# Where a language-model tower prepares its FFN weights: raw loads into the bytes of the result, in-place mixing, the token chain first, and half of the turning moved into FFN block 0

## The chip, the cores and the metric

One NeuronCore of one Trainium2 chip. The metric is the device time of one execution in microseconds; the median of three runs is given. The profiled execution is a run of its own, with its own time.

## The reference, cut to what matters

16 rows of 256 token ids below 128 go through one tower. All ids come from a table of 128 rows, so everything up to the attention scores depends on the table alone.

```python
h = rms(rms(emb[x], norm_weight) @ proj.T)                    # token part: 128 distinct rows
y = layernorm(h);  q, k, v = y @ Wq.T, y @ Wk.T, y @ Wv.T     # 16 heads of 32
q, k = layernorm(q*gamma + beta), layernorm(k*gamma + beta)   # per head
attn = tril((q k^T / sqrt(32)) ** 2)
h = h + (attn @ v / (rowsum(attn) + 1e-5)) @ Wo.T
x = fwht512(layernorm(h) * SU_ug) / 64                        # Walsh-Hadamard transform
x = silu(x @ W_gate.T * ws_g) * (x @ W_up.T * ws_u)           # W_gate, W_up: 2048 x 512
x = fwht2048(x * SU_dp) / 64
h = h + x @ W_down.T * ws_d                                   # W_down: 512 x 2048
```

## The kernel before

The 4096 tokens are eight blocks of 512. Work is written as five instruction streams (SP issues loads, POOL, DVE, ACT, PE), and each stream's order is written out by hand. Semaphores named in the code order the streams against each other; a stream that waits holds back all that is behind it.

**Preparation.** SP loads the weights. PE turns (transposes) the 128x128 tiles of `proj`, Wq, Wk, Wv, Wo with `small_unit` (20 units of four tiles; each unit goes through one PSUM bank and is copied by ACT with `small_copy`, in two banks `TURN_SMALL` used in turn). The token part, q, k and v of the 128 rows, and the scores follow; ACT squares the scores and writes their high fp16 half, DVE the low half (`att`). Every fp32 weight of the large products is kept as two fp16 halves, so a product is three matmuls (`split_mm`, lines 1009 to 1011).

W_gate and W_up are eight groups of 512 rows, 32 units of four tiles. A group first needs the sums of squares of its rows (`gu_squares` on ACT, line 778: four 128x512 squares), `gu_norm` (DVE), a power on POOL (line 302), `gu_scale` (DVE, which also builds a diagonal matrix), and then PE multiplies the raw tiles with that diagonal (`turn_unit`, line 1004), ACT copies the high half (line 781) and DVE subtracts to get the low half (`unit`, line 438). W_down is mixed along its 2048 columns by four butterfly stages on DVE for each of its four row groups (`down_mix`, 16 mixes, each two `tensor_tensor` of 128x1024 at lines 410 and 411, from one buffer to another), turned (`down_turn`, 16 units), multiplied with a 128x128 Hadamard matrix (`down_hada`, line 1040) and split into halves (`down_unit`).

**Slots.** A block's attention is 32 slots and its FFN is 32 slots. In attention slots 0 to 15 each slot handles one head: PE picks (`PICK`, lines 1138, 1139), DVE multiplies with the counts (`product`, line 633), ACT writes the high half, POOL the low half (line 337). After heads 3, 7, 11, 15 (slots 4, 8, 12, 15, `SUMS_AT`) PE sums over four heads (line 1153), DVE divides (lines 642 to 651), ACT and POOL split, and a slot or two later PE flips the result and ACT copies it (`oT`). From slot 18 on PE multiplies with Wo; per 128 tokens DVE adds the residual (line 675), takes the norm, mixes by butterflies (lines 687, 410, 411), ACT and DVE split (`x16`, line 660), PE flips and applies the Hadamard matrix, ACT and DVE split again into `xT` (line 667). FFN slots 0 to 15 compute gate and up (`feed_half`), slots 16 to 31 the product with W_down (`feed_down`).

Block 0's attention runs alone, with the units and mixes of the weights between its slots (`UNITS_IN_SLOT`, `DOWN_MIX_AT`). After it, block b's FFN runs beside block b+1's attention: FFN block 0 is written out (with the 16 `down_turn` and 16 `down_hada` in its slots 0 to 8), blocks 1 to 6 are a hardware loop on each engine, and FFN block 7 runs alone. In FFN block 0 gate and up have one PSUM bank each (`GATE0`, `UP0`), and banks 2 and 3 (`D_TURN`, `D_HADA`) serve the turning.

The raw FFN weights land in other buffers that are free by then: `raw = HID + WD` (the hidden activations and the later W_down halves), and W_down's rows wait for such buffers with `norm_load`.

Of the kernel before, what the change touches and what calls it, by code (L numbers as in the profile page):

```python
# [13 lines left out]
P = 128  # L14
# [20 lines left out]
def units_of_slot(s):  # L35
    first = EARLY + sum(UNITS_IN_SLOT[:s])
    return list(range(first, first + UNITS_IN_SLOT[s]))


NORM_FROM = 15  # L40
BOUND_AT = 24


def down_turns(p):
    return [p] if p < 16 else []


def down_evicts(p):
    return [p - 1] if 1 <= p < 17 else []


def tower(nc, x, emb, norm_w, proj_w, wq, wk, wv, wo, gamma, beta, su_ug, su_dp, wsc_ug, wsc_dp,
# [28 lines left out]
    with ctx:  # L81
# [9 lines left out]
        wgu = sb("wgu", [P, GROUPS, 2, DC, 512], F16)  # L91
        wd = sb("wd", [P, DC, 2, FT, P], F16)
# [44 lines left out]
        gl = sb("gl", [P, 8])  # L137
        k_o, k_d, s_w = gl[:, 0:1], gl[:, 1:2], gl[:, 6:7]


        def words(v):
# [4 lines left out]
        WD = [words(wd[:, i, :, :, :].rearrange("p a b c -> p (a b c)")) for i in range(DC)]  # L146
# [3 lines left out]

        raw = HID + WD
        small_raw = [v.rearrange("p (a b) -> p a b", a=4) for v in (XT, P16, H1A, GU[4], GU[5])]
        small_t = [v.rearrange("p (a b) -> p a b", a=4) for v in (OT, GU[6], GU[7], GU[3])]
        emb_s, embn, nw_b, h_tok = [WD[2][:, 512 * i:512 * i + 512] for i in range(4)]
        x1, xTf, qk = WD[3][:, 0:512], WD[3][:, 512:1024], WD[3][:, 1024:2048]
        qk2, ones = XT[:, 0:1024], late[:, 0:128]
        qkT = GU[6][:, 0:1024]
        sq = GU[7].rearrange("p (a b) -> p a b", a=4)
# [5 lines left out]
        gu_diags = [a_diag, v_diag]  # L164
# [4 lines left out]

        mixX, mixY = HID[1], HID[3]  # L170
        down_path = [[WD[0], mixX, WD[0], mixX, WD[2]],
                     [WD[1], mixX, WD[1], mixX, WD[3]],
                     [mixY, mixX, mixY, mixX, mixY],
                     [HID[0], HID[2], mixX, WD[2], mixX]]
        norm_raw = [WD[0], WD[1], mixY, HID[0]]
# [8 lines left out]
        TURN = banks[0:4]  # L184
        GATE0, UP0, D_TURN, D_HADA = banks[0], banks[1], banks[2], banks[3]
        SUMS = banks[3]
        TURN_SMALL, VT, PROJ, QKV, SCORE = banks[4:6], banks[6], banks[7], [banks[7], banks[6], banks[5]], banks[4:8]


        names = """c_land e_land p_land w_land0 w_land1 w_land2 w_land3 par_land h_stored  # L190
        gu_land0 gu_land1 gu_land2 gu_land3 gu_land4 gu_land5 gu_land6 gu_land7
# [7 lines left out]
        n_land0 n_land1 n_land2 n_land3 d_ss d_mix d_diag e_ready e_sum e_pow sc_ready  # L199
# [11 lines left out]


# [5 lines left out]
        def _(sp):  # L218
            def quarters(w):
                return w.rearrange("(c p) d -> p c d", p=P)  # L220

            nc.sync.dma_start(late[:, 1536:1792], c_square).then_inc(S["c_land"], 16)
            nc.sync.dma_start(emb_s, emb).then_inc(S["e_land"], 16)
            nc.sync.dma_start(nw_b, rows(norm_w, D)).then_inc(S["e_land"], 16)
            nc.sync.dma_start(small_raw[0], quarters(proj_w)).then_inc(S["p_land"], 16)
            for i, w in enumerate((wq, wk, wv, wo)):
                nc.sync.dma_start(small_raw[1 + i], quarters(w)).then_inc(S[f"w_land{i}"], 16)
# [3 lines left out]
            def gu_load(n):  # L231
                w, g = (w_up if n % 2 else w_gate), n // 2
                nc.sync.dma_start(raw[n].rearrange("p (a b) -> p a b", a=4), quarters(w[512 * g:512 * g + 512, :]))\
                    .then_inc(S[f"gu_land{n}"], 16)

            for n in range(6):
                gu_load(n)
            sp.wait_ge(S["x1_ready"], 1)
            sp.wait_ge(S["h_stored"], 16)
            gu_load(6)  # L240
            sp.wait_ge(S["v_ready"], 1)
            sp.wait_ge(S["feat_ready"], 1)
            gu_load(7)

            def norm_load(dt, turned):
                sp.wait_ge(S["turned"], turned)
                nc.sync.dma_start(norm_raw[dt], w_down[dt * P:(dt + 1) * P, :]).then_inc(S[f"n_land{dt}"], 16)

            norm_load(3, 4)
# [41 lines left out]
        def _(pool):  # L291
# [12 lines left out]
            def gu_power(n):  # L304
                c = slice(column(n), column(n) + 4)
                pool.wait_ge(S["gu_rn"], n + 1)
                power(rn[:, c], ss[:, c]).then_inc(S["gu_pow"], 1)


            pool.wait_ge(S["pow_asked"], 1)  # L310
            power(stat[:, 1:2], stat[:, 0:1]).then_inc(S["pow_given"], 1)
            pool.wait_ge(S["pow_asked"], 2)
            power(stat[:, 3:4], stat[:, 2:3]).then_inc(S["pow_given"], 1)
# [12 lines left out]
            def prepare(u):  # L326
                n = u // 4 + 3
                if u % 4 == 3 and n < GROUPS:
                    gu_power(n)

            for u in range(EARLY):
                prepare(u)

# [990 lines left out]
```

## Time and profile before

| | |
|---|---|
| median of 3 runs | 1439.61 us (1438.97 to 1442.25) |
| profiled execution, its own time | 1439.44 us |
| its span, first to last instruction | 1437.6 us |
| PE / DVE / ACT / POOL busy | 93% / 36% / 32% / 29% |
| mean granted TensorE clock | 0.97 |

The device time stands 1.8 us above the span. Busy shares are means over stages with different limits. Times in the rows are from the start of the span. The profiler prints for each row the start, the length, the engine, the line and what is written from what.

### The profile page before, as it was taken

To read this page: it belongs to the slowest core of one execution; us is meant where nothing else is said; L and a number is where in the kernel's file an instruction comes from. 1 tells how busy PE (TensorE), PEld (TensorE's weight loads), DVE (VectorE), ACT (ScalarE), POOL (GpSimd) and SP (SyncE) were. 2 spreads that over 40 slices of the span, in tenths; PEclk is the share of its full clock that TensorE was granted. 3 is DMA by queue.
4 is the path that set the end of the run, shared out by engine and by line. 5 is a ranking of instruction groups with operands and counts; after the bars stand their busy time and mean duration, and the time that the engine had idled before them with its cause. 6 is when DMAs were issued, how large, how long until landed. Compare 5 with 4: busy or idle time off the path is not lost.

```text
span 1437.6 us, 20304 instructions
## 1 busy us (share of the span) xinstructions
PE 1331.6 (93%) x7989; PEld 673.4 (47%) x7989; DVE 524.0 (36%) x1039; ACT 457.4 (32%) x767; POOL 418.1 (29%) x372
## 2 busy tenths in 40 slices
PE   5566439998999999999999999999999999999998
PEld 3455215554444544544444444444445445444444
DVE  1456695322522252224322442234322622251110
ACT  3475424432224312331234123322332224312220
POOL 0234212233134322442134214331343224420210
PEclk9889769999999999999999999999999999999999
DMA  9211000000100010001000010001000100010000
GB/s 332 93 61 67 22 8 1 1 1 22 38 8 1 8 45 16 1 1 47 21 0 1 30 38 1 1 23 38 8 0 9 44 16 1 1 45 15 1 1 30
DMA packets 21453, 39.41 MB, mean 27 GB/s; under 512 B 6212, under 2 KB 6520, under 8 KB 20856
## 3 DMA queue, kind: packets, MB, share of 16 engines
q1 hardware_dynamic: 17856, 28.99, 5.8%
q0 software_dynamic: 2560, 8.39, 2.0%
q8 instruction: 72, 1.18, 0.3%
q10 hardware_dynamic: 952, 0.75, 0.2%
q14 instruction: 13, 0.11, 0.0%
HBM read 29.47 MB, written 8.65 MB: 27 GB/s over the span
## 4 chain that ended last, share of the span: by engine, by line
PE 88%; DVE 6%; ACT 3%; issue 1%; DMA 1%; POOL 0%; SPq 0%; DVEq 0%; ACTq 0%
PE bank L1009 25%; PE bank L1010 25%; PE bank L1011 25%; PE bank L1153 3%; PE bank L1004 2%; PE bank L1138 2%; PE bank L1139 2%; ACT sg L778 2%; DMA wgu<-in_L_attn_Wv 1%; PE bank L1040 1%; PE bank L1173 1%; PE bank L1163 1%; PE bank L1002 1%; PE bank L1078 0%; DVE hid L410 0%
## 5 line engine op out<-in xcount | busy, mean ns | idle before, releaser
L1009 PE MATMUL bank<-xT,wgu 128*128 128x512 f16 x1024 | 389.1, 380 | 4.2 <-DVE xT L667 4.2
L1010 PE MATMUL bank<-xT,wgu 128*128 128x512 f16 x1024 | 389.1, 380 | 0.0
L1011 PE MATMUL bank<-xT,wgu 128*128 128x512 f16 x1024 | 389.1, 380 | 0.0
L365 POOL TENSOR_TENSOR hid<-a,hid 128x512 f16<-128x512 f32 x128 | 147.8, 1155 | 518.3 <-ACT hid L781 518.3
L701 DVE SCALAR_TENSOR_TENSOR a<-bank,kap,sg 128x512 f32<-128x512 f32 x128 | 96.1, 750 | 517.2 <-PE bank L1011 360.3
L1011 PE MATMUL bank<-wd,hid 128*128 128x512 f16 x512 | 194.8, 381 | 0.0
L1010 PE MATMUL bank<-wd,hid 128*128 128x512 f16 x512 | 194.8, 381 | 0.0
L1009 PE MATMUL bank<-wd,hid 128*128 128x512 f16 x512 | 194.8, 380 | 0.0
L337 POOL TENSOR_TENSOR p<-prod,p 128x512 f16<-128x512 f32 x128 | 149.0, 1166 | 133.8 <-ACT p L781 133.8
L781 ACT ACTIVATE hid<-a 128x512 f16<-128x512 f32 x128 | 80.6, 630 | 277.2 <-DVE a L701 277.2
L1011 PEld LDWEIGHTS bank<-xT,wgu 128*128 128x128 f16 x1024 | 100.3, 98 | 121.4 <-issue 1.1
L1009 PEld LDWEIGHTS bank<-xT,wgu 128*128 128x128 f16 x1024 | 100.3, 98 | 121.0 <-DVE xT L667 5.1
L1010 PEld LDWEIGHTS bank<-xT,wgu 128*128 128x128 f16 x1024 | 100.3, 98 | 115.3 <-issue 1.2
L932 ACT ACTIVATE sg<-bank,sc 128x512 f32<-128x512 f32 x128 | 87.2, 681 | 128.9 <-PE bank L1011 72.7
L781 ACT ACTIVATE p<-prod 128x512 f16<-128x512 f32 x128 | 79.6, 626 | 124.5 <-PE bank L1153 111.4
L781 ACT ACTIVATE sg<-wide,rstd 128x512 f16<-128x512 f32 x32 | 23.1, 722 | 229.1 <-DVE wide L411 229.1
L633 DVE TENSOR_TENSOR prod<-bank,cnt 128x512 f32<-128x512 f32 x128 | 86.5, 680 | 12.2 <-ACT cnt L781 12.2
L302 POOL TENSOR_TENSOR rstd<-ve,mhalf 128x1 f32<-128x1 f32 x32 | 32.5, 1015 | 199.3 <-DVE ve L684 199.3
L1011 PEld LDWEIGHTS bank<-wd,hid 128*128 128x128 f16 x512 | 50.3, 98 | 60.9 <-issue 0.8
L1009 PEld LDWEIGHTS bank<-wd,hid 128*128 128x128 f16 x512 | 50.3, 98 | 58.4 <-issue 0.8
L1010 PEld LDWEIGHTS bank<-wd,hid 128*128 128x128 f16 x512 | 50.3, 98 | 58.4 <-issue 0.8
L675 DVE SCALAR_TENSOR_TENSOR h<-bank,gl,h_row 128x512 f32 (+1 forms) x32 | 24.0, 750 | 101.5 <-PE bank L1011 101.5
(181 smaller groups left out, 1365.3 us busy)
## 6 DMA issues: line engine op xcount, KB each, us to landing
out<-a SPq DMA_DIRECT2D x24, 256.0 KB, 2.1
ids_b<-in_x SPq DMA_DIRECT2D x8, 256.0 KB, 4.0
hid<-in_L_ffn_W_gate SPq DMA_DIRECT2D x2, 1024.0 KB, 11.8
hid<-in_L_ffn_W_up SPq DMA_DIRECT2D x2, 1024.0 KB, 12.8
wd<-in_L_ffn_W_gate SPq DMA_DIRECT2D x2, 1024.0 KB, 11.7
wd<-in_L_ffn_W_up SPq DMA_DIRECT2D x2, 1024.0 KB, 10.1
hid<-in_L_ffn_W_down SPq DMA_DIRECT2D x2, 1024.0 KB, 4.8
wd<-in_L_ffn_W_down SPq DMA_DIRECT2D x2, 1024.0 KB, 4.8
```

Source lines behind the costliest of these rows:

```text
L302: return nc.gpsimd.tensor_tensor(dst, src, mhalf[:, 0:src.shape[1]], ALU.pow)
L337: nc.gpsimd.tensor_tensor(p16[:, 1, h % 4, :], prod[:, h % 2, :], p16[:, 0, h % 4, :], ALU.subtract)\
L365: nc.gpsimd.tensor_tensor(hid[:, 1, s, :], a32[:, :], hid[:, 0, s, :], ALU.subtract)\
L633: nc.vector.tensor_tensor(prod[:, s % 2, :], PICK[s % 2][:, :], cnt[:, :], ALU.mult)\
L701: nc.vector.scalar_tensor_tensor(a32[:, :], bank[:, :], kap[:, s:s + 1], sg[:, :], ALU.mult, ALU.mult).then_inc(S["a_done"], 1)
L778: nc.scalar.activation(sg[:, :], src, ACT.Square, accum_out=dst).then_inc(S[name], 1)
L781: return nc.scalar.activation(dst, src, ACT.Copy, **kw)
L932: nc.scalar.activation(sg[:, :], bank[:, :], ACT.Silu, scale=sc[:, s:s + 1]).then_inc(S["silu_done"], 1)
L1009: mm(dst, w[0], v[0], start=first, stop=False)
L1010: mm(dst, w[0], v[1], start=False, stop=False)
L1011: return mm(dst, w[1], v[0], start=False, stop=final)
L1153: last = mm(HEADS[m // 2][:, 4 * (m % 2) + j, :], p16[:, p, j, m * P:(m + 1) * P], val[:, w, 4 * q + j, :], start=first, stop=final, skip_ ...
```

## The change

1. **Layout and raw loads.** `wgu` and `wd` are laid out so that the fp16 halves made from a raw unit occupy the bytes of that unit. Raw gate and up groups load into `wgu` itself, W_down's rows into `wd` itself, all early in SP's stream. A gate or up group is now four DMAs with pieces of 512 B on the SBUF side, where it was one DMA with pieces of 2 KB.
2. **In-place mixing.** `down_mix` writes `a - b` over b, waits for that, then writes `2a - (a - b)` over a. Its pieces: two mixes ahead of slot 0, fourteen in FFN block 0's slots 1 to 13.
3. **Token chain first.** The embedding table is loaded first and turned first; `small_unit` has four banks; q and k signal one by one and their per-head norms (`features`) run one after the other; ACT's squares of Wv and the gate and up groups move behind the token chain; the score squares are interleaved with their copies; the ids come earlier; block 0's four indirect row reads go straight into `h1` before slot 0.
4. **Units.** 16 of the 32 gate and up units are turned in attention slots 2 to 17 of block 0, one a slot, none before slot 0 is reached; the other 16 in FFN block 0's slots 0 to 7, two a slot, through the bank `D_TURN`. The 16 W_down units move from FFN slots 0 to 8 to FFN slots 8 to 16.
5. **Norms in pairs.** A gate and an up group are normed by one `pair_norm`, `pair_power`, `pair_scale`; the bound that scales the activations is taken in two halves (`half_terms`, `half_scale`), the second half and W_down's scale (`fit_terms`, `fit_scale`) in FFN block 0's slots 4 to 7. The squares of groups 6 and 7 and of half of W_down's rows are taken on ACT in FFN slots 0 to 5.

```diff
-EARLY = 8
-UNITS_IN_SLOT = (1, 1, 2, 1, 1, 1, 2, 1, 1, 1, 2, 1, 1, 1, 2, 1, 1, 1, 1, 1) + (0,) * 12
-DOWN_MIX_AT = (18, 19, 20, 21, 22, 23, 24, 25, 26, 27, 28, 29, 30, 31, 34, 35)
+BEFORE = 16
+UNITS_IN_SLOT = (0, 0) + (1,) * BEFORE + (0,) * 14
+UNITS_BESIDE = 16
+NORM_AT = {4: 1, 24: 2}
+SCALE_AT = {6: 1, 26: 2}
+DIAG_AT = {6: (2,), 10: (3,), 26: (4,), 27: (5,)}
+BOUND_AT = 17
+MIXED_BEFORE = 2
+MIX_BESIDE = (1, 2, 3, 4, 5, 6, 7, 8, 9, 10, 11, 12, 12, 13)
...
-        wgu = sb("wgu", [P, GROUPS, 2, DC, 512], F16)
-        wd = sb("wd", [P, DC, 2, FT, P], F16)
+        wgu = sb("wgu", [P, GROUPS, DC, 2, 512], F16)
+        wd = sb("wd", [P, DC, FT // 4, 2, 4, P], F16)
...
+            def gu_load(n):
+                w, g = (w_up if n % 2 else w_gate), n // 2
+                for i in range(4):
+                    rows_of_tile = w[512 * g + P * i:512 * g + P * i + P, :].rearrange("p (k d) -> p k d", k=DC)
+                    nc.sync.dma_start(raw[n][:, :, i, :], rows_of_tile).then_inc(S[f"gu_land{n}"], 16)
...
             def down_mix(k):
...
-                a, c = [halves(v, P << st) for v in down_path[dt][st:st + 2]]
-                butterfly(c, a).then_inc(S["d_mix"], 1)
+                v = halves(WD[dt], P << k % 4)
+                if k % 4:
+                    dve.wait_ge(S["d_mix"], k)
+                link(nc.vector.tensor_tensor(v[:, :, 1, :], v[:, :, 0, :], v[:, :, 1, :], ALU.subtract))
+                nc.vector.scalar_tensor_tensor(v[:, :, 0, :], v[:, :, 0, :], 2.0, v[:, :, 1, :], ALU.mult, ALU.subtract)\
+                    .then_inc(S["d_mix"], 1)
...
@@ ACT, attention slots of block 0 @@
-                for u in us[:1]:
-                    unit(u)
...
                 x_high(0, s)
                 product(0, s)
+                if s < 2:
+                    wo_high(2 * s)
+                    wo_high(2 * s + 1)
+                for u in units_of_slot(s):
+                    unit(u, TURN[u % 4])
                 attend(0, s)
@@ PE, FFN block 0 @@
                     feed_half(s, 0, GATE0, S["gate_ready"])
                     for v in down_evicts(2 * s):
                         down_hada(v)
+                    for u in units_beside(2 * s):
+                        turn_beside(u)
                     for v in down_turns(2 * s):
                         down_turn(v)
...
+            def turn_beside(u):
+                pe.wait_ge(S["w_lo"], u)
+                turn_unit(u, D_TURN)
@@ DVE, FFN block 0 @@
+                for u in units_beside(2 * s):
+                    unit(u, D_TURN)
                 for v in down_evicts(2 * s):
                     down_unit(v)
                 feed(0, s, UP0)
+                for u in units_beside(2 * s + 1):
+                    unit(u, D_TURN)
```

## Rows read from the trace of the kernel before

**Rows 1.** Busy us by stage: PE PEld DVE ACT POOL; then clock, DMA share, GB/s.

```profile
0.00:91.70 91.70, 50.49 (x276) 39.28 (x277) 32.11 (x83) 46.16 (x104) 15.15 (x16) 0.85 0.49 179
91.70:156.20 64.50, 41.92 (x434) 31.57 (x433) 38.70 (x78) 43.56 (x98) 27.26 (x24) 0.89 0.17 58
156.20:208.40 52.20, 17.55 (x78) 7.72 (x76) 50.13 (x91) 10.63 (x17) 9.95 (x8) 0.69 0.05 15
208.40:397.20 188.80, 184.86 (x1084) 96.68 (x1085) 76.59 (x131) 65.22 (x102) 50.79 (x44) 0.97 0.04 12
397.20:549.20 152.00, 152.00 (x925) 73.62 (x924) 51.78 (x106) 45.12 (x69) 49.42 (x44) 1.00 0.05 17
```

**Rows 2.** Timeline of the preparation, 31 to 65 us.

```profile
31.64 7.13 PE L1078 MATMUL bank<-wgu,wd 128*128 128x512 f32 x16 [0.74 <-ACT wd L781]
49.82 1.29 DVE L578 TENSOR_TENSOR wd<-bank,cnt 128x512 f32<-128x512 f32 x2
59.04 5.43 POOL L302 TENSOR_TENSOR cnt<-cnt,mhalf 128x32 f32<-128x32 f32 x1 [0.68 <-DVE cnt L589]
```

**Rows 3.** The chain that ended last: one of the squares of weights on ACT.

```profile
43.68 0.73 ACT sg L778 x2
```

**Rows 4.** Timeline of attention slots, block 0: a product and a unit, then a sum.

```profile
108.94 0.68 DVE L633 TENSOR_TENSOR prod<-bank,cnt 128x512 f32<-128x512 f32 x1
109.66 0.63 ACT L781 ACTIVATE p<-prod 128x512 f16<-128x512 f32 x1 [0.43 <-DVE prod L633]
110.81 0.57 ACT L781 ACTIVATE wgu<-bank 128x512 f16<-128x512 f32 x1
112.07 0.67 DVE L633 TENSOR_TENSOR prod<-bank,cnt 128x512 f32<-128x512 f32 x1
...
137.00 0.68 DVE L633 TENSOR_TENSOR prod<-bank,cnt 128x512 f32<-128x512 f32 x1
...
139.63 1.38 PE L1153 MATMUL bank<-val,p 128*128 128x33 f16 x48 [2.34 <-POOL p L337]
...
141.77 0.76 DVE L651 TENSOR_TENSOR wide<-bank,zr 128x256 f32<-128x256 f32 x2 [0.20 <-DVE zr L647]
```

**Rows 5.** Timeline from the product with Wo on, two residuals.

```profile
151.23 0.61 PE L1009 MATMUL bank<-wo_t,oT 128*128 128x512 f16 x1 [6.13 <-ACT oT L781]
156.22 0.75 DVE L675 SCALAR_TENSOR_TENSOR h<-bank,gl,h_row 128x512 f32<-128x512 f32 x1 [0.79 <-PE bank L1011]
160.44 1.22 DVE L410 TENSOR_TENSOR hid<-wd 128x1024 f32<-128x1024 f32 x1
160.60 0.72 ACT L781 ACTIVATE sg<-wide,rstd 128x512 f16<-128x512 f32 x1 [2.36 <-DVE wide L411]
166.24 0.74 DVE L675 SCALAR_TENSOR_TENSOR h<-bank,gl,h_row 128x512 f32<-128x512 f32 x1
```

**Rows 6.** Timeline of FFN block 0.

```profile
222.65 1.02 PE L1040 MATMUL bank<-h 128*128 128x512 f32 x2
223.50 1.05 PE L1004 MATMUL bank<-h,wd 128*128 128x128 f32 x8
224.40 0.38 PE L1009 MATMUL bank<-xT,wgu 128*128 128x512 f16 x1
...
226.99 1.02 PE L1040 MATMUL bank<-h 128*128 128x512 f32 x2
...
240.18 2.18 DVE L411 TENSOR_TENSOR wd<-hid 128x1024 f32<-128x1024 f32 x1
...
338.17 1.55 PE L1153 MATMUL bank<-val,p 128*128 128x33 f16 x48 [3.90 <-POOL p L337]
```

**Rows 7.** ACT's table loads, all there are (count, then busy and mean).

```profile
L778 ACT ACT_TABLE_LOAD x1 | 1.3, 1283 | 6.6 <-issue 6.6
L932 ACT ACT_TABLE_LOAD x1 | 1.3, 1283 | 8.9 <-PE bank L1011 8.9
```

**Rows 8.** Page, DMA queues: packets, MB, share of 16 engines.

```profile
q10 hardware_dynamic: 952, 0.75, 0.2%
```

More of the change, by code:

```diff
@@ L236, in _ @@
-            for n in range(6):
-                gu_load(n)
[L238 to L249, printed above, removed]
@@ L345, in attend @@
                         .then_inc(S["ol_done"], 1)
-                if s in ROWS_AT:
+                if s in ROWS_AT and not first(n):
                     m = ROWS_AT.index(s)
@@ L505, in ids, with down_scale @@
+            def down_scale():
+                dve.wait_ge(S["turned"], UNITS)
+                for i in range(4):
+                    last = nc.vector.tensor_scalar(d_diag[:, i, :], ident, ws_d[:, i:i + 1], None, ALU.mult)
+                last.then_inc(S["d_diag"], 1)
             def ids(n):
@@ L603, in _ @@
[L603 to L612 removed]
+            pair_scale(0)
+            group_diag(0)
             att_v = att[:, :, :, :].rearrange("p l (q j) v -> p l j q v", j=4)
@@ L744, in _ @@
                 attend(1, s)
-                for k in range(16):
-                    if DOWN_MIX_AT[k] == s + SLOTS:
-                        down_mix(k)
+                if s == NORM_BESIDE:
+                    pair_norm(3)
+                if s == SCALE_BESIDE:
+                    pair_scale(3)
+                for n in DIAG_BESIDE.get(s, ()):
+                    group_diag(n)
+                if s == BOUND_BESIDE:
+                    half_terms(1)
+                if s == BOUND_BESIDE + 1:
+                    bound_low(1)
+                if s == BOUND_BESIDE + 2:
+                    half_scale(1)
+                if s == FIT_BESIDE:
+                    fit_terms()
+                if s == FIT_BESIDE + 1:
+                    bound_low(2)
+                if s == FIT_BESIDE + 2:
+                    fit_scale()
+                    down_scale()
+                for i, at in enumerate(MIX_BESIDE):
+                    if at == s:
+                        down_mix(MIXED_BEFORE + i)
             finish(0, 3)
@@ L830, in _ @@
                 square_sum(st4[:, rt:rt + 1], small_raw[4][:, rt, :], "wo_sq")
-            gu_squares(0)
-            gu_squares(1)
+            act.wait_ge(S["h_stored"], 16)
+            act.wait_ge(S["score_ready"], 1)
+            att_v = att[:, :, :, :].rearrange("p l (q j) v -> p l j q v", j=4)
+            for j in range(4):
+                nc.scalar.activation(sq[:, j, :], SCORE[j][:, :], ACT.Square).then_inc(S["a_sq"], 1)
+                act.wait_ge(S["a_sq"], j + 1)
+                copy(att_v[:, 0, j, :, :], sq[:, j, :].rearrange("p (q v) -> p q v", v=P), scale=32.0).then_inc(S["a_hi"], 1)
             act.wait_ge(S["v_ready"], 1)
             copy(val[:, 0, :, 0:DH], QKV[2][:, :].rearrange("p (h d) -> p h d", d=DH), scale=V_TOP).then_inc(S["v_hi"], 1)
-            unit(0)
-            unit(1)
             def wo_high(k):
@@ L967, in _ @@
                 feed_high(0, s)
+                for u in units_beside(2 * s + 1):
+                    unit(u, D_TURN)
                 for v in down_evicts(2 * s + 1):
@@ L1200, in feed_half @@
                 for k in range(DC):
-                    last = split_mm(bank[:, :], [wgu[:, n, l, k, c] for l in range(2)],
+                    last = split_mm(bank[:, :], [wgu[:, n, k, l, c] for l in range(2)],
                                     [xT[:, l, k, :] for l in range(2)], k == 0, k == DC - 1)
```

689 lines of the change are left out of this document (356 added, 333 removed).

## The prediction

> **What bounds the kernel now.** I read the busy time by stage first [rows 1]. The stages part at the first product (91.7), the first residual add (156.2), the first gate matmul of FFN block 0 (208.4) and that of block 1 (397.2). From there PE has no gap: a loop block takes 152.0 with PE busy 152.0. The six loop blocks and the last FFN are 1437.6 - 397.2 = 1040.4 us, and their matmuls have the same shapes and counts afterwards (the new strides of `wgu` and `wd` still give 128 adjacent halves a piece), so I leave them as they are. What can move is the first 397.2 us, of which PE idles 91.7 - 50.5, 64.5 - 41.9, 52.2 - 17.6 and 188.8 - 184.9 us. The end follows the time at which block 1 starts, one for one.
>
> Which wait ends last, by stage: the preparation is a chain through ACT's squares and DVE's norms of q and k [rows 2, 3]; slots 0 to 17 are a round of DVE, ACT and POOL [rows 4]; from 156.2 DVE is busy 50.1 of 52.2, largely with the old mixes; FFN block 0 is PE's but for one idle stretch of 3.90 [rows 6].
>
> **1. Preparation, until the first product: 91.7 becomes 66.5.** The Q and K products began at 31.6, when ACT had copied the turned vector [rows 2]; ahead of that copy in ACT's queue stood four squares of Wv (4 x 0.73, [rows 3]) and copies through two banks. Without the squares and with four banks I put the start at 28.0, after 0.6 to 0.9 for the later norm weight. (The norm weight now loads behind `proj`; that is the delay.) Q and K products take 7.13 for both [rows 2]: Q ends at 31.7, K at 35.2. The norm of q and k started only at 49.8, behind squares of Wo; now it starts with Q. A step over 512 elements is 0.65 (1.29 for two), six such and two short ones are 4.4 per half, so it ends at 40.6. The power over 32 columns took 5.43; over 16 I take half, 2.9, and the first of the two lies under the second half. Then `v_diag`, 1.3: PE goes on at 41.9 after 6.7 us of idling, partly at its lower clock: three units, two turns, the scores: 49.0. One more unit and copy (1.6), Wo's squares (2.9), four pairs of square and copy in turn (5.1), the last low half (0.8): 59.4. Then on DVE, ahead of the first product, v's low half, a diagonal, two short steps (1.8) and two in-place mixes. A mix was 2.4 (two of 1.22, [rows 5]); the second op is now a `scalar_tensor_tensor`, and there is a wait between. No row has one of 1024 elements; from below it is another 1.22, from above two residual adds of 0.75 [rows 5] and 0.1 for the wait. I take 2.6 a mix, 5.2 for two: 66.5. Gain 25.2, bounds 18 to 31. The four indirect reads on POOL stand ahead of its first product; they start about 60, when POOL is free, and end with DVE's mixes; uncovered they would cost up to 4 us.
>
> **2. Slots 0 to 15: 45.3 becomes 50.5.** The first product to the sixteenth was 91.7 to 137.0. Now ACT copies a product's high half before a unit's, and both lie between DVE's product and DVE's unit: a round of 0.72 from product to ACT, 0.54 to the unit's copy, 1.26 from there to the next product, 2.52 together [rows 4]. Before, the unit's copy ran ahead, and a slot without a wait was 1.2. So this edit loses. A sum holds the next products: 2.63 from the product to the sum, 2.9 more to the end of the division [rows 4], then ACT, POOL, a flip and a copy in series; walked through the queues a group of four heads takes 12.65, against 11.8 on average before. Slots 0 to 3 with four units of Wo and four squares: 9.7. Three groups: 38.0. Pair norm, scale and two diagonals: 2.8. Loss 5.2; nothing at best (the ACT squares that stood between the slots are gone), 9 at worst.
>
> **3. Last product to first residual: 19.2 becomes 14.2.** 137.0 to 156.2 held twelve of W_down's squares on ACT ahead of the last copy. Now: sum and division 5.4, split 1.9, flip and copy 1.9, Wo at the lower clock 5.0 (151.2 to 156.2, [rows 5]). Gain 5.0, bounds 3 to 7. `half_terms` lies under it; with no cover it would be 1.9.
>
> **4. First residual to FFN block 0: 52.2 becomes 30.5.** A residual followed the last by 10.0 (156.22 to 166.24), of which two mixes were 2 x 2.4. Without them: 4.3 to the end of the butterflies (160.60), 0.8 for ACT's half, 0.7 for DVE's; for the third and fourth PE's Wo at the lower clock ends later still. I place the four at 0, 5.9, 11.8 and 17.8, the last low half ends at 23.7, and flip, copy, Hadamard (waiting for the one before) and split take 6. I add 0.8 for W_down's squares on ACT. Gain 21.7, bounds 17 to 25.
>
> **5. FFN block 0: 188.8 becomes 207.0.** In 188.8 are a loop block (152.0), 16 Hadamards of 0.85 and 16 units of 0.90 [rows 6] (28.0), gate 0 at the lower clock (2.6), the idle 3.9 and what the clock lost there. Sixteen more units are 16 x 0.90 = 14.4. The idle stretch after slot 15's up is filled by a Hadamard and a unit, -1.75. Then the new pressure on DVE in slots 1 to 7, where PE needs 7.4 a slot (gate and up 2 x 2.59, 224.40 to 226.99; two units 1.80; a pick of two matmuls 0.43). DVE has product, two units, an activation (2.8) and a mix. The only mixes that ran beside POOL's subtractions had an op of 2.18 instead of 1.22 [rows 6]: 3.5 a mix. From a unit's turn through ACT (0.75), the unit (0.6), the mix (3.5), the next product (0.7), the next unit (0.6) to the end of the next turn (1.0) is 7.15 already, and slots 4 to 7 add 1.3 for a sum, 1.9 for `half_terms`, about 2.5 for diagonal and `fit_terms`, 1 for `half_scale`, 2.5 to 4 for `fit_scale` and `down_scale`. I take 5.5 of stalls. With no collision (2.4 a mix) it is 1, with every mix and short step held by POOL 13 or more. What is late when DVE is late is `D_TURN`'s next unit, then up. From slot 8 PE needs 9.1 and DVE's 6.4 is covered. Loss 18.2, bounds 13 to 27.
>
> **The loads** cost nothing in the sum: the mix needs its rows at 61, gate groups 2 and 3 are squared from 67, groups 4 and 5 after 117. At the 48 ns that a packet of mixed sizes took (0.2% of 16 x 1437.6 over 952, [rows 8]) a MB in 512 B pieces is 2048 / 16 x 48 = 6.1 us: group 1 lands near 35, the last near 80. Still under cover.
>
> **Sum.** -25.2 + 5.2 - 5.0 - 21.7 + 18.2 = -28.5. The profiled execution's 1439.4 (0.17 below the median) becomes 1411. With the bounds partly offsetting each other this case spans 1401 to 1424.
>
> **A. That case, 76 in 100: 1411.** Against it: every walk through queues leaves out waits.
>
> **B. Given back in FFN block 0, 11 in 100: 1422.** Each of 14 mixes and some fifteen short steps is held by about 1 us; only half of that is covered: 11 more than A. For it: the 2.18. Against it: two rows only, and the other op of the same mixes kept 1.22.
>
> **C. Table loads on ACT, 7 in 100: 1420.** ACT loads a table before its first square and before its first Silu, 1.28 each [rows 7]. The new order alternates squares and Silu in FFN slots 0 to 5. Were squares not served by Silu's table, that is 12 more loads, 15.4 us of ACT, of which with ACT at 6.2 of 7.4 in slots 0 and 1 about 9 reach PE. Against: copies ran after either load and needed none. The Trainium skill, ScalarE: Activation LUTs, "Table sets: the hidden batching unit", says to batch calls by set and puts a switch at about 2.7 us with its drain, which would make it an estimated 18 to 25 us on the path; it also says that cheap functions are in every set but does not name square there. The two rows fit both readings.
>
> **D. FFN block 0 falls to the lower clock, 4 in 100: slower, 1447.** PE's granted clock was 0.69 in the stage of long gaps [rows 1], and the sum after the idle 3.90 took 1.55 where another took 1.38 [rows 4, 6]. At the lower level a slot costs 5.2 + 1.5 = 6.7 more. If DVE's lateness made such gaps in slots 1 to 7, all seven cold are 47, less 11 already counted as stalls: 1447. It decides from five cold slots (34 against the 28.5). Against: my gaps are 1 to 3 us, and PE is fed within each slot.
>
> **E. Late weights, 2 in 100: slower, 1440.** At 24 us a MB, four times the bound of [rows 8], group 1 would land at 70 instead of 35, and all behind its squares 30 later.
>
> **Range.** 1400 to 1424 leaves out D, E, the upper half of B and C, and an eighth of A. "Same" means within 0.2%, 2.9 us, about what a measurement of this kernel can tell. Faster 0.94 (A, B, C and some of D), same 0.01, slower 0.05.
>
> **What would show it.** After: first product near 66, sixteenth near 117, first residual near 131, first gate matmul near 162, block 1 near 369, and loop blocks of 152.0. Products 2.5 apart in slots 5 to 7 and 9 to 11. No new table load. DVE over 85% busy in FFN slots 4 to 7 and PE waiting there on DVE (line of `unit`) 1 to 3 us at a time, at clock 1.00. I am wrong if the first gate matmul comes after 175, or if FFN block 0 takes over 216, or if the loop block isn't 152.

## The result, and the profile after

The changed kernel takes 1420.12 us (median of 4 executions, 1419.58 to 1421.55) where the kernel before took 1439.7; the ratio is 0.9862 (95% interval 0.9845 to 0.988). The prediction said 1411 with a range of 1400 to 1424. The profiled execution took 1420.2, its span is 1418.4. One execution of a kernel further down ("gaps filled") took 1465 at a granted clock of 0.93 and is left out everywhere.

The busy time by stage, cut at the same events as [rows 1] (first product, sixteenth product, first residual, first gate matmul, block 1, one loop block); the columns are those of [rows 1]:

```profile
0.00:68.50 68.50, 38.77 (x187) 26.28 (x187) 27.14 (x64) 30.58 (x67) 14.51 (x15) 0.90 0.92 291
68.50:118.80 50.30, 33.70 (x321) 28.12 (x322) 26.67 (x59) 28.07 (x54) 24.13 (x21) 0.83 0.07 19
118.80:132.80 14.00, 7.54 (x76) 4.42 (x76) 5.11 (x18) 5.68 (x12) 2.38 (x3) 0.63 0.00 0
132.80:166.80 34.00, 15.90 (x78) 7.09 (x78) 23.54 (x55) 16.12 (x35) 6.25 (x6) 0.73 0.00 1
166.80:378.30 211.50, 201.79 (x1216) 112.64 (x1217) 123.22 (x200) 85.67 (x154) 61.42 (x47) 0.98 0.03 11
378.30:530.30 152.00, 152.00 (x925) 73.70 (x924) 51.82 (x106) 45.14 (x69) 49.40 (x44) 1.00 0.05 17
```

| stage | before | predicted | after |
|---|---|---|---|
| 1, to the first product | 91.7 | 66.5 | 68.5 |
| 2, to the sixteenth | 45.3 | 50.5 | 50.25 |
| 3, to the first residual | 19.2 | 14.2 | 14.0 |
| 4, to the first gate matmul | 52.2 | 30.5 | 34.0 |
| 5, FFN block 0 | 188.8 | 207.0 | 211.5 |
| all behind it | 1040.4 | 1040.4 | 1040.1 |

Every stage moved the way it was forecast; the missing 9 us lie in stages 1, 4 and 5. The kernel is 19.6 us faster where 28.5 were forecast. The end of the preparation, which answers to [rows 2] (start, length, engine, line, what is written from what):

```profile
28.99 8.83 PE L1153 MATMUL bank<-wd,hid 128*128 128x512 f32 x16 [0.69 <-ACT hid L835]
...
61.46 0.69 DVE L624 SCALAR_TENSOR_TENSOR att<-hid,att 128x512 f16<-128x512 f32 x1 [0.46 <-ACT att L835]
...
63.53 1.22 DVE L471 TENSOR_TENSOR wd<-wd 128x1024 f32<-128x1024 f32 x1
64.78 1.22 DVE L472 SCALAR_TENSOR_TENSOR wd<-wd 128x1024 f32<-128x1024 f32 x1
...
66.81 0.41 PE L1205 MATMUL bank<-onehotT,att 128*128 128x512 f16 x1
...
68.52 0.68 DVE L654 TENSOR_TENSOR prod<-bank,cnt 128x512 f32<-128x512 f32 x1
```

Two things are to be seen. Q and K took 8.83 in one piece, 1.70 more than the 7.13 of [rows 2], for the same sixteen matmuls. The granted clock was 0.57 from 28.99 to 33.00 us and 1.00 from there. And the picks were done at 67.2, so the mixes held the first product by little more than a microsecond, not by their 5.

The slots, which answer to [rows 4]: product, its high half, the unit's high half, the unit's low half, and only then the next product.

```profile
76.04 0.69 DVE L654 TENSOR_TENSOR prod<-bank,cnt 128x512 f32<-128x512 f32 x1 [0.68 <-PE bank L1205]
76.77 0.63 ACT L835 ACTIVATE p<-prod 128x512 f16<-128x512 f32 x1 [0.91 <-DVE prod L654]
77.30 0.58 ACT L835 ACTIVATE wgu<-bank 128x512 f16<-128x512 f32 x1
...
77.91 0.69 DVE L457 TENSOR_TENSOR wgu<-bank,wgu 128x512 f16<-128x512 f32 x1 [1.18 <-ACT wgu L835]
...
78.52 0.68 DVE L654 TENSOR_TENSOR prod<-bank,cnt 128x512 f32<-128x512 f32 x1
```

The residuals, which answer to [rows 5], came at 132.81, 138.57, 144.38 and 152.12. This is what lay ahead of the fourth:

```profile
148.25 0.42 DVE L429 TENSOR_TENSOR wide<-prod 128x256 f32<-128x256 f32 x1
148.70 0.72 ACT L835 ACTIVATE sg<-wide,rstd 128x512 f16<-128x512 f32 x1 [2.81 <-DVE wide L429]
...
150.23 0.59 ACT L835 ACTIVATE xT<-bank 128x512 f16<-128x512 f32 x1
...
150.85 0.69 DVE L688 TENSOR_TENSOR xT<-bank,xT 128x512 f16<-128x512 f32 x1 [2.19 <-ACT xT L835]
...
151.46 0.74 DVE L681 SCALAR_TENSOR_TENSOR sg<-wide,rstd,sg 128x512 f16<-128x512 f32 x1
...
152.12 0.74 DVE L697 SCALAR_TENSOR_TENSOR h<-bank,gl,h 128x512 f32<-128x512 f32 x1
```

From 148.7 DVE waits 2.19 for ACT's high half of `xT` (line 688), while the low half of `x16` (line 681), whose input ACT had ready at 149.4, and the residual stand behind it.

In FFN block 0 (the groups by line; then the timeline at slot 12, which answers to [rows 6]):

```profile
L472 DVE SCALAR_TENSOR_TENSOR wd<-wd 128x1024 f32<-128x1024 f32 x14 | 23.0, 1644 | 0.5
L471 DVE TENSOR_TENSOR wd<-wd 128x1024 f32<-128x1024 f32 x14 | 18.2, 1297 | 0.0
L1062 PE MATMUL bank<-h,wgu 128*128 128x128 f32 x128 | 17.9, 284 | 2.5 <-DVE wgu L457 1.7 <-DVE h L451 0.7
L1062 PE MATMUL bank<-h,wd 128*128 128x128 f32 x128 | 17.8, 285 | 1.8 <-DVE h L528 1.8
```

```profile
287.67 1.77 DVE L471 TENSOR_TENSOR wd<-wd 128x1024 f32<-128x1024 f32 x1
288.49 1.96 POOL L359 TENSOR_TENSOR h_row<-wide,h_row 128x512 f16<-128x512 f32 x1
...
289.47 2.06 DVE L472 SCALAR_TENSOR_TENSOR wd<-wd 128x1024 f32<-128x1024 f32 x1
291.57 1.22 DVE L471 TENSOR_TENSOR wd<-wd 128x1024 f32<-128x1024 f32 x1
292.83 1.23 DVE L472 SCALAR_TENSOR_TENSOR wd<-wd 128x1024 f32<-128x1024 f32 x1
...
295.46 1.96 PE L1110 MATMUL bank<-h 128*128 128x512 f32 x2 [2.12 <-DVE wd L479]
...
297.21 1.90 PE L1062 MATMUL bank<-h,wd 128*128 128x128 f32 x8
```

In seven of the fourteen mixes the second op began while a POOL op ran and took 2.06 or 2.07: those of slots 1, 2 and 8 to 11 and the first of slot 12. In the others, those of slots 3 to 7 among them, it took 1.22 or 1.23. Behind the idle 2.12 the Hadamard product took 1.96 (1.02 elsewhere) and the unit 1.90 (1.05 elsewhere): PE was at its lower level there.

PE idles 9.7 of 211.5: 5.0 up to 246 us (five waits of 0.55 to 0.69 and one of 1.83, all for DVE), 2.1 behind the pair of mixes in slot 12, 2.6 before the sum behind slot 15. ACT's table loads (instructions that load the tables of its functions), which answer to [rows 7], are still two, although squares (line 832) and Silu (line 982) now alternate:

```profile
L832 ACT ACT_TABLE_LOAD x1 | 1.3, 1283 | 5.0 <-issue 5.0
L982 ACT ACT_TABLE_LOAD x1 | 1.3, 1283 | 4.0 <-PE bank L1069 4.0
```

### The profile page after: what moved, and what is told of

It reads as the page before. It is cut to its first block, busy times and chain, and to the rows that moved or that the text cites. A ratio compares the mean times of both kernels' runs of the same rounds, so it can differ in the third digit from the quotient of the medians.

```text
span 1418.4 us, 20319 instructions
## 1 busy us (share of the span) xinstructions
PE 1334.5 (94%) x7993; PEld 676.7 (48%) x7993; DVE 532.4 (38%) x1049; ACT 458.0 (32%) x767; POOL 423.6 (30%) x371
## 3 DMA queue, kind: packets, MB, share of 16 engines
q1 hardware_dynamic: 30528, 28.99, 6.3%
## 4 chain that ended last, share of the span: by engine, by line
PE 89%; DVE 5%; ACT 3%; issue 1%; POOL 1%; DMA 1%; SPq 0%; DVEq 0%; ACTq 0%
PE bank L1067 25%; PE bank L1068 25%; PE bank L1069 25%; PE bank L1219 3%; PE bank L1062 2%; PE bank L1204 2%; PE bank L1205 2%; PE bank L1229 1%; PE bank L1110 1%; PE bank L1239 1%; DMA hid<-in_L_tok_norm_weight 1%; PE bank L1060 1%; DVE wgu L457 1%; PE bank L1247 0%; PE bank L1248 0%
## 5 line engine op out<-in xcount | busy, mean ns | idle before, releaser
L338 POOL TENSOR_TENSOR p<-prod,p 128x512 f16<-128x512 f32 x128 | 153.2, 1199 | 135.8 <-ACT p L835 135.7
L697 DVE SCALAR_TENSOR_TENSOR h<-bank,gl,h_row 128x512 f32 (+1 forms) x28 | 21.0, 751 | 98.0 <-PE bank L1069 97.2
```

The costliest lines, as they stand in the source:

```text
L338: nc.gpsimd.tensor_tensor(p16[:, 1, h % 4, :], prod[:, h % 2, :], p16[:, 0, h % 4, :], ALU.subtract)\
```

## The experiments

The changed kernel ran once more and eleven others ran, each beside the kernel before (median 1438 to 1440). The changed kernel stood beside "unit's copy first", "mixes moved" and "two mixes late" only; the others are set against it across groups of runs, in which the median of the kernel before moved by 2. Times of stages are from the profiled executions; "start" is the start of PE's Q product.

| kernel | median (lowest, highest) | start | first product | 16th | first gate | FFN block 0 |
|---|---|---|---|---|---|---|
| changed, first timing | 1420.1 (1419.6, 1421.6) | 28.99 | 68.52 | 118.77 | 166.79 | 211.5 |
| changed again | 1415.7 (1414.0, 1421.2) | 28.97 | 67.05 | 117.27 | 165.40 | 208.3 |
| unit's copy first | 1412.7 (1411.0, 1414.0) | 27.71 | 67.33 | 111.23 | 159.07 | 211.5 |
| mixes moved | 1415.7 (1414.4, 1417.9) | 29.14 | 68.89 | 119.12 | 167.25 | 208.7 |
| two mixes late | 1415.6 (1413.2, 1418.0) | 29.76 | 67.40 | 116.98 | 165.66 | 210.3 |
| picks first | 1411.2 (1410.3, 1413.1) | 27.30 | 60.30 | 109.78 | 158.56 | 210.1 |
| low half of `xT` late | 1416.0 (1415.3, 1416.6) | 28.75 | 66.70 | 116.94 | 162.05 | 211.3 |
| mixes left out | 1411.2 (1410.2, 1415.9) | 28.16 | 67.61 | 117.84 | 165.83 | 207.9 |
| norm weight first | 1417.6 (1413.1, 1418.3) | 25.71 | 63.93 | 114.11 | 162.32 | 208.4 |
| Wv's squares first | 1420.4 (1418.3, 1422.9) | 32.07 | 70.25 | 120.46 | 168.68 | 208.3 |
| gaps filled | 1415.6 (1411.4, 1416.2) | 28.84 | 67.17 | 117.27 | 165.16 | 208.6 |
| all parts | 1401.6 (1400.3, 1403.8) | 26.34 | 59.62 | 103.55 | 149.99 | 208.3 |
| all parts, gaps filled | 1398.9 (1397.0, 1400.7) | 26.45 | 59.70 | 103.62 | 149.23 | 207.8 |

The start of Q varies without any edit ahead of it: 27.3 to 29.8, mean 28.6, in the nine traces in which the norm weight's place and Wv's squares are those of the changed kernel. With it varies the landing of the norm weight, 9.4 to 11.6 after its issue. So a difference of one or two microseconds in the columns up to the first gate is worth reading only from the start of Q on.

**The changed kernel again.**

> The changed kernel itself, run beside the next three on the same chip, so that they can be set against it. 1420 us, as in its first timing.

```profile
28.97 7.13 PE L1153 MATMUL bank<-wd,hid 128*128 128x512 f32 x16 [0.69 <-ACT hid L835]
```

It took 1415.7, and its five executions fall into two levels: 1414.0, 1415.6, 1415.7 and 1420.6, 1421.2. With the first timing there are three low and six high; the mean of the nine is 1418.7. The profile is of a low one, and set against the first it shows where the 4.6 between them lie: Q and K took 7.13 instead of 8.83; the first 11 us of gate and up had a granted clock of 0.88 instead of 0.73 (1.6, counted to the second Silu); from the Silu of slot 13 to that of slot 14, where the idle behind the mixes of slot 12 lies, it took 11.92 instead of 13.58 (1.7). (The expectation for "gaps filled" below calls this stretch slot 12 to slot 13.) No other stretch differs by more than 0.4. These are stretches at PE's lower level that are now there, now not (Q and K had a granted clock of 1.00 here), so a median here can move by 4 us with no edit, and the stages say more.

**The unit's copy first.**

> One part of the change undone: in block 0's attention slots ACT copies the unit's high half before the product's. In the changed kernel the slots came 2.5 us apart (product 76.04, 78.52, 80.99) and the first to the sixteenth product took 50.25. Theory (step 2 of the prediction: the loss comes from this order, since both copies now lie between DVE's product and DVE's unit): rounds of about 2.1, the stretch near 45, and 1415 us (1412 to 1417). Rival (the sums, with POOL's low halves behind them, set the pace of a group of four heads, and the order only fills the wait): rounds shrink but the next sum comes no earlier, the stretch stays above 48.5, and the time is 1418 to 1420.

```diff
                 x_high(0, s)
+                for u in units_of_slot(s):
+                    unit(u, TURN[u % 4])
                 product(0, s)
                 ...
-                for u in units_of_slot(s):
-                    unit(u, TURN[u % 4])
```

First to sixteenth product: 43.9 for 50.25. The theory holds, and its 5 was too small: 6.3. The timeline shows the unit's copy at 77.49 done before the product's, and the next product 1.90 behind the last:

```profile
76.81 0.69 DVE L654 TENSOR_TENSOR prod<-bank,cnt 128x512 f32<-128x512 f32 x1 [0.66 <-PE bank L1205]
...
77.49 0.58 ACT L835 ACTIVATE wgu<-bank 128x512 f16<-128x512 f32 x1
77.97 0.62 ACT L835 ACTIVATE p<-prod 128x512 f16<-128x512 f32 x1
78.10 0.69 DVE L457 TENSOR_TENSOR wgu<-bank,wgu 128x512 f16<-128x512 f32 x1 [0.60 <-ACT wgu L835]
...
78.71 0.68 DVE L654 TENSOR_TENSOR prod<-bank,cnt 128x512 f32<-128x512 f32 x1
```

**The fourteen mixes elsewhere, and left out.**

> The fourteen mixes in FFN block 0 are placed elsewhere: two right after block 0's attention slot 31, the others one a slot in FFN slots 0, 1, 2, 3, 5, 6 and 8 to 13, so none in slots 4 and 7 and no pair in slot 12. The changed kernel idled 9.7 us of PE in this stage: 1.25 up to 209.5 us, 3.7 in 209.5 to 246, 4.75 in 246 to 330, of which 2.1 stood before DVE's work behind the double mix. Theory (the stalls come from where DVE's long steps meet the mixes, step 5): FFN block 0 takes 205 to 207 where it took 211.5, 1414 us (1412 to 1416). Rival (what holds DVE is that every short step beside POOL's operations is stretched, wherever the mixes are): 209.5 to 211.5 and 1418 to 1420.

The two mixes of slot -1 stand behind attention slot 31.

```diff
-MIX_BESIDE = (1, 2, 3, 4, 5, 6, 7, 8, 9, 10, 11, 12, 12, 13)
+MIX_BESIDE = (-1, -1, 0, 1, 2, 3, 5, 6, 8, 9, 10, 11, 12, 13)
```

> The fourteen mixes in FFN block 0 work on 8 columns of one half-pair instead of 2 x 1024 elements each: this kernel leaves out the mixing of W_down but for the two mixes ahead of slot 0, and so measures what mixing beside the FFN costs. In the changed kernel PE idled 9.7 us in this stage. Theory (step 5: the stalls come from DVE having a mix in each slot): the idle falls to 2 or 3 us and the time to 1409 (1407 to 1411) beside 1416. Rival (the mixes are covered but for the pair in slot 12, and the stalls of slots 4 to 8 are the chains of short steps around the sums, scales and diagonals themselves): idle 7 or more, 1413 to 1415.

```diff
                 v = halves(WD[dt], P << k % 4)
+                if k >= MIXED_BEFORE:
+                    v = v[:, 0:1, :, 0:8]
```

This second kernel leaves out nearly all mixing of W_down, so it doesn't compute what the reference does. From one Silu to the next, in us, from that of slot 3 to that of slot 8 and from that of slot 11 to that of slot 15 (read from ACT's timeline):

| kernel | 3 to 4, and on to 8 | 11 to 12, and on to 15 |
|---|---|---|
| changed | 7.56, 10.25, 9.10, 8.57, 7.74 | 9.11, 10.31, 13.58, 9.11 |
| changed again | 7.54, 10.25, 9.11, 8.57, 7.74 | 9.11, 10.32, 11.92, 9.11 |
| mixes moved | 7.56, 10.26, 8.54, 8.76, 7.74 | 9.10, 10.32, 9.55, 9.52 |
| mixes left out | 7.40, 10.40, 8.54, 7.88, 7.45 | 9.11, 10.31, 9.55, 9.11 |

The pair in slot 12 cost 2.4, and 4.0 where it took PE to the lower level; both kernels without it have 9.55. From slot 3 to slot 8 leaving out every mix gives 1.5, moving those of slots 4 and 7 away 0.4. The 3.7 idle from 209.5 to 246 stays 3.2 without any mix, and the whole idle is 7.3, as the rival of "mixes left out" had it; its theory (2 or 3) falls. PE's two waits of 0.60 behind a mix are gone there, but 2.11 remain before the first unit of W_down, at the end of DVE's short steps of the scales. It is only the pair that a better place removes.

The times say less. "Mixes moved" has its median, 1415.7, in the theory's range, but FFN block 0 at 208.7, between theory (205 to 207) and rival (209.5 to 211.5). 1.1 of that is another stretch at the lower level: behind the idle 2.6 before the sum of slot 15 the next Hadamard product took 1.95, where it took 1.10 in the changed kernel. The same stretch is low in "two mixes late", "picks first" and both kernels with all parts. The median without mixes, 1411.2, is 1.8 below the rival's range and just above the theory's. Its FFN block 0 is 207.9 with one lower-clock slot in it (slot 8 to 9: 13.47 for 11.5); without that it would be about 206, an estimate from these two.

**The norm weight first.**

> One part undone: the norm weight is loaded ahead of proj, as in the kernel before. In the changed kernel it landed at 13.0, in the chain that ended last, and proj at 10.15. Theory (step 1 had 0.6 to 0.9 for this delay): the first product comes 0.6 to 1.5 earlier, 1415 us beside 1416. Rival (proj then lands later by as much and PE's first turns wait for it): no change.

```diff
-            nc.sync.dma_start(small_raw[0], quarters(proj_w)).then_inc(S["p_land"], 16)
             nc.sync.dma_start(nw_b, rows(norm_w, D)).then_inc(S["nw_land"], 16)
+            nc.sync.dma_start(small_raw[0], quarters(proj_w)).then_inc(S["p_land"], 16)
```

The norm of the table, in "changed again" and here:

```profile
13.42 0.75 DVE L555 SCALAR_TENSOR_TENSOR hid<-hid,cnt 128x512 f32<-128x512 f32 x1 [5.79 <-DMA hid<-in_L_tok_norm_weight]
```

```profile
9.93 0.75 DVE L555 SCALAR_TENSOR_TENSOR hid<-hid,cnt 128x512 f32<-128x512 f32 x1 [0.83 <-POOL cnt L312]
```

The norm weight landed 6.9 after its issue instead of 11.3, `proj` 9.4 instead of 8.6, and all from Q on came 3.1 to 3.3 earlier than in "changed again". Some of this is the spread of the start of Q. The three traces with the norm weight first ("all parts" and "all parts, gaps filled" too) have Q at 25.7, 26.3 and 26.5, the nine others at 28.6 in the mean: about 2.5. That is still more than twice what the theory had; the rival (no change) falls. The mean of its four executions is 2.1 below that of the changed kernel; three of them stood 4 to 5 above the profiled one.

**Wv's squares first.**

> One part undone: the four squares of Wv stand on ACT ahead of the copies of small units 4 to 11 again, as they did before. Theory (step 1: ACT's squares ahead of the token chain are what the preparation gained): the Q product begins 2 to 3 later than 29.0, and so does all behind it, 1419 to 1420 beside 1416 to 1418.7. Rival (ACT has room there, since the norm weight's landing at 13.0 and the matmuls of proj end last): no change.

The four squares stood at 23.81 to 26.6, copies and turns behind them, and Q began at 32.07: 3.1 later, the first product 3.2 later, 1419.5 for the profiled execution against 1415.6. Counted from the norm of the table, which waits for the norm weight, Q began 18.4 later, and 15.3 to 16.4 later in the others: about 2.5 for the squares. The theory holds.

**The two mixes late, and the picks first.**

> The two mixes ahead of attention slot 0 move to slot 17, where DVE waits for the last heads and for Wo. In the changed kernel they ran from 63.53 to 68.5 and the first product followed. Theory (the mixes are all that lay between the scores and the first product, as the sum of step 1 has it): the first product comes near 63.6, 5 earlier, and 1415 us. Rival (POOL's four indirect reads, which stood at 65.35 to 70.8 ahead of POOL's first low half, take over): the first products come early, but POOL's low halves and with them the first sum come at most 1.5 to 3 earlier, 1417 to 1419. In neither case should the first residual be late through the mixes at slot 17.

```diff
-            for k in range(MIXED_BEFORE):
-                down_mix(k)
             for s in range(SLOTS):
                 ...
                 if s == BOUND_AT:
                     half_terms(0)
+                    for k in range(MIXED_BEFORE):
+                        down_mix(k)
```

From the start of Q to the first product it took 37.64; the changed kernel took 39.53 with Q and K at the same 8.83. The two mixes were worth 1.9, not 5, so the theory falls although its 1415 came out (the median is 1415.6); and the rival that I had named, POOL, was not what came next. The first residual was 0.4 to 0.5 late through the mixes at slot 17, which the expectation had ruled out. What came next was PE: `[3.00 <-PE bank L1205]` stands at the first product.

```profile
63.61 0.66 PE L1060 MATMUL bank<-h,hid 128*128 128x128 f32 x4 [4.47 <-DVE val L627]
64.10 1.77 PE L1062 MATMUL bank<-a,wgu 128*128 128x128 f32 x8
...
67.40 0.69 DVE L654 TENSOR_TENSOR prod<-bank,cnt 128x512 f32<-128x512 f32 x1 [3.00 <-PE bank L1205]
```

> Follows from the run with the two mixes in slot 17, where the first product came only 1.1 earlier: PE's queue was next, with a unit of Wo that waited for v's low half (63.56), a unit of eight matmuls at the lower clock, then the counts and the picks of heads 0 and 1, released at 66.3 to 67.6. Here the mixes are in slot 17, the counts and picks stand ahead of those two units, and POOL's four indirect reads stand behind its work of slots 13, 14, 16 and 17. Theory (these three together are what lies between the scores' low halves, done at 62, and the first product; the mixes alone were not the term of 5.2 that step 1 has): first product at 64.5 to 65, POOL's first low half within 2 us of it, the sixteenth product 3 to 5 earlier, 1412 us beside 1416. Rival (slots 0 and 1 with Wo's four units set the pace whatever the first product does): sixteenth product at most 1.5 earlier, 1414.5 to 1416.

```diff
                     small_unit(16 + 2 * s)
+                    if s == 0:
+                        attend(0, 0)
                     small_unit(17 + 2 * s)
```

(The moved mixes, as above, and POOL's moved reads are not printed.) From the start of Q to the first product it now takes 33.00, 5.1 less than "changed again" (both with Q and K at 7.13), and it is 5.2 less to the first residual, though the mixes cost 0.6 in slot 17. The theory holds, and was too small: the sixteenth product came 5.8 earlier from the start of Q, for 3 to 5. The first product at 60.3 for 64.5 to 65 owes 1.7 to a Q that began that much earlier. The three edits were made together, so their shares are not shown. The median is 1411.2, the mean of the changed kernel's nine executions 1418.7.

**The low half of `xT` later.**

> In block 0's attention DVE takes the low half of xT one step later: for the first 128 tokens behind the fourth residual add, for the others behind the low half of x16 in slot 26 and at the end of slots 28 and 30. In the changed kernel DVE stood idle 2.19 us before the xT low half at 150.85 and 2.10 before the one at 158.59, each time with the low half of x16 (ready at 149.4 and 157.2) queued behind it; the fourth residual came 7.7 after the third where the two before came 5.8 apart. Theory (this order is what made stage 4 longer than the prediction had it, 34.0 instead of 30.5): the fourth residual comes 6 after the third, and from the first residual to the first gate matmul it is 29.5 to 31; 1412 us beside 1416 of the changed kernel. Rival (the ring through PE, ACT's 1.00 us copy and the one bank of the Hadamard product is as long as DVE's): 32.5 to 34, 1415 to 1416.

```diff
                     nc.vector.scalar_tensor_tensor(row, WOUT[m % 2][:, :], k_o, resid, ALU.mult, ALU.add)\
                         .then_inc(S["h1_done"], 1)
+                    if first and m == 3:
+                        xt_low(n, 0)
                     ...
+                if first and s in (26, 28, 30):
+                    xt_low(n, (s - 24) // 2)
```

(The old place is passed over in block 0's attention; that part is not printed.)

```profile
146.93 0.72 ACT L842 ACTIVATE sg<-wide,rstd 128x512 f16<-128x512 f32 x1 [2.81 <-DVE wide L429]
...
147.68 0.75 DVE L688 SCALAR_TENSOR_TENSOR sg<-wide,rstd,sg 128x512 f16<-128x512 f32 x1 [0.79 <-ACT sg L842]
148.35 0.74 DVE L700 SCALAR_TENSOR_TENSOR h<-bank,gl,h 128x512 f32<-128x512 f32 x1
...
149.08 0.69 DVE L661 TENSOR_TENSOR xT<-bank,xT 128x512 f16<-128x512 f32 x1
```

The four residuals are 5.76, 5.81 and 5.74 apart, and the stage takes 31.0 for 34.0. The theory holds for the stage. For the time (1412) it missed: the median, 1416.0, is below the mean of the changed kernel but not below its low level; its profile had FFN block 0 at 211.3, with slot 13 to 14 at 13.53 and the first gates at 0.75.

**PE's gaps filled.**

> The changed kernel, with matmuls of no use (128x512 fp16 into a bank that is free there) in PE's gaps ahead of FFN block 0: eleven ahead of the last turn of x16 (a gap of 5.86), four ahead of the last Hadamard product (2.48), two behind it (1.42). In the traces so far the first 11 us of gate and up ran at a granted clock of 0.73 to 0.88 after these gaps, and slot 12 to slot 13, behind an idle 2.1, took 13.58 in the traces with 0.73 and 11.92 in those with 0.88; the nine executions of the changed kernel stand at 1414.0 to 1415.7 (three) and at 1419.6 to 1421.6 (six). Theory (the clock is low there because PE was idle before, step 5's term of 2.6): with the gaps filled the first 11 us run at 0.95 or more, FFN block 0 takes 206 to 208, and every execution is at 1412 to 1415. Rival (the clock follows something else than the last few us of PE): 0.73 to 0.88 again, and both levels again.

```profile
163.16 0.38 PE L1250 MATMUL bank<-prod,hada 128*128 128x512 f16 x1 [1.10 <-DVE xT L688]
...
165.16 0.61 PE L1067 MATMUL bank<-xT,wgu 128*128 128x512 f16 x1 [0.98 <-DVE xT L688]
```

The Hadamard product at 163.16 ran at 0.38 where it was 0.59 ahead of the last gap in the changed kernel, so the filling did raise the clock; but two microseconds later the first gate matmul took 0.61 again, and the first 11 us had 0.85, FFN block 0 208.6. The theory (0.95, 206 to 208) falls in the form that I gave it: PE had gaps of only 1.10 and 0.98 there and fell back all the same. All five executions stood at 1411.4 to 1416.2, none on the high level; without the changed kernel beside them this doesn't show that the filling did it.

**All parts.**

> All six edits together: the unit's copy first in attention slots, norm weight first, the two mixes in slot 17 with the indirect reads and the picks moved, the fourteen mixes elsewhere, the low half of xT later. If the stages add up: preparation 56.5 to 60, sixteenth product 44 to 45 later, 14 to 15 to the first residual, 31 to the first gate matmul, FFN block 0 207 to 210; 1395 to 1401. If each edit's gain was another's wait: 1405 to 1408.

> The six edits and PE's gaps ahead of FFN block 0 filled as well (eight, four and two matmuls). If the clock theory holds, 2 to 4 below the run of the six edits without them; otherwise the same, or 1 slower where the matmuls stand in the way.

1401.6, half a microsecond above the range for adding stages: first product at 59.6, 43.9 for the slots, 15.4 to the first residual (the two mixes in slot 17 ended at 118.98, just as the residual was due), 31.0, 208.3. With the gaps filled too, 1398.9, a ratio of 0.972 (0.9696 to 0.9743) to the kernel before. With those matmuls the stretch from first residual to first gate ran at 0.88 for 0.76 and took 0.8 less, and the first 11 us of gates ran at 0.87 for 0.75; FFN block 0 took 0.5 less. The medians are 2.7 apart. So the filling is worth 1.3 in the traces and 2.7 in the medians, for the 2 to 4 that were expected. In the traces it gave 0.8 ahead of the gates and 1.3 up to the third Silu, and 0.9 was lost again at the stretch behind slot 15, where the lower level lasted longer here.

## Why the prediction was right, and where its terms were off

**The number.** The stages were off by +2.0, -0.25, -0.2, +3.5, +4.5 and -0.3, which takes 1411 to 1420.2. That is nearer the 1422 of B and the 1420 of C than the 1411 of A, but neither of their mechanisms made it: it is case A with 9 us less gain.

**Step 1, +2.0.** Of "token chain first" the squares of Wv were put back by themselves, and measure 2.5 to 3.1, near the 4 x 0.73 of the prediction; what the other squares and the earlier norms of q and k are worth, no run shows alone. "0.6 to 0.9 for the later norm weight" was mis-sized: it measures about 2.5. I had priced one transfer behind another and not what the queues of `proj` and the weights take together. The rest of that sum was about 1 too large, so Q came 1.0 late. Then Q and K took 8.83 for 7.13, partly at the lower level, and PE went on at 45.09 for 41.9, 3.2 late (idle 7.28 for 6.7). What follows was luck: "three units, two turns, the scores: 49.0" ended at 57.7, 12.6 after PE went on for 7.1, at a clock of 0.74 up to the scores; but Wo's squares, which I had placed behind the scores, ran beside them from 53.87, and from the scores' end to the last low half it was 4.4 for 10.4. The errors of 5.5 and 6.0 cancel. The two mixes took 5.0, near the 5.2 that I gave them, but they were no term of the path in that size: 1.9 was, since PE's turns and picks, which I had not walked, end right before them.

**Step 2, right, 50.25 for 50.5.** The mechanism is shown: with the order undone 43.9. So the rest of the change made this stage 1.4 faster than before, and the order alone costs 6.3. The sign "2.5 apart in slots 5 to 7 and 9 to 11" came only by half: the second step of each was 4.3 and 3.9, since scale and diagonals, which the sum had as 2.8 apart, stand there.

**Step 3, right,** 14.0 for 14.2.

**Step 4, +3.5.** "I place the four at 0, 5.9, 11.8 and 17.8": they came at 0, 5.8, 11.6 and 19.3, and the last low half ended at 27.1 for 23.7; the 6.8 from there to the gates were right. What failed is the walk through DVE's queue: it left out that the low half of `xT` stands ahead of the low half of `x16`, and waits for ACT there. Moving it gave 31.0.

**Step 5, +4.5.** Of this 2.1 are stalls: 9.7 idle where I had 5.5 and the rest of the old 3.90, 2.15. The failing sentence is "From slot 8 PE needs 9.1 and DVE's 6.4 is covered": it counts one mix a slot, and slot 12 has two (idle 2.1). Another 1.7 is that PE ran at the lower level behind it, from slot 13 to slot 14. The first gates at 0.73 cost about 3.0 of 11.0 (11.0 x 0.27) for my 2.6. The 5.5 up to slot 8 were 5.0 by luck, not for the reason given: the walk of 7.15 a slot rested on mixes of 3.5, those of slots 3 to 7 took 2.5, and leaving all mixes out removes only 1.5 there. DVE was 79% busy in slots 4 to 7 where I had over 85, and PE waited 0.6 to 1.8 at a time where I had 1 to 3, at clock 1.00 as said.

**The rivals.** B (held steps) is half there: line 472 averages 1.64, 0.42 above 1.22, not 1, as 7 of the 14 were held by 0.84. In "mixes left out" ops on 8 columns were held as well (five of 28 took 0.72 to 1.05 in place of 0.16). C is dead: two table loads. The Trainium skill's rule (ScalarE: Activation LUTs, "Table sets: the hidden batching unit") to batch calls by set has nothing to gain here, since square and Silu alternated with no load between. D is not there: slots 1 to 7 ran at clock 1.00. Its mechanism is there behind slot 12 (and in some traces behind slot 15), one slot long and not seven. E is dead: queue 10's price of 6.1 us a MB was on the safe side, as SP issued the last six groups of gate and up, 1 MB each, within 27 us, 4.5 us each, with two other weights queued just ahead of them.

## What to carry to other kernels

Walk every hand-ordered queue by its issue order at the point where two interleaved streams meet: one instruction that waits for another engine ahead of a ready one cost 6.3 in the slots and 3.0 between the residuals, and a changed order gave each back. A term that lies "ahead of" the next step in one queue counts only by what it exceeds the other queues that the step needs as well. When an execution can fall on two levels, compare stages between traces, not medians.

## What the runs showed of the hardware

- TensorE's two levels can fall differently on the same instructions in executions of the same kernel: sixteen fp32 matmuls took 8.83 (granted clock 0.81) or 7.13 (1.00), the first 11 us of gates had 0.73 or 0.88, and nine executions stood at 1414.0 to 1415.7 or 1419.6 to 1421.6. The Trainium skill, TensorE: Matmul & The Clock Gate, "What's actually happening", says that the same kernel shows different counts of slow matmuls from run to run; the traces agree.
- A DVE op with two SBUF operands of 1024 fp32 beside a POOL op took 1.77 to 2.07 instead of 1.22 where the POOL op had begun first, and an op on 8 columns up to 1.05 instead of 0.16. POOL's op took up to 2.25 instead of 1.16; in slot 13 it began second and took 2.00, and the DVE op kept its 1.23. The Trainium skill, GPSIMD Engine Reference, "Specifications", names contention with DVE instructions that have two SBUF inputs; the traces agree.
- 256 KB issued behind 1 MB landed 9.4 to 11.6 after their issue (ten traces), ahead of it 6.9 to 7.6 (three), while the 1 MB took 8.1 to 9.4 in front and 9.4 to 10.3 behind.
- With the DMA engines busy all the time, the gate and up weights in pieces of 512 B came in at 295 GB/s (34 to 50 us of the changed kernel, packets of 541 B in the mean), and in pieces of 2 KB at 388 GB/s (24 to 40 us of the kernel before, 1958 B).
